# RWKV block times routed experts: rounded count sums, an earlier table load, a split wait, a reordered step

## The reference, cut to what matters

```
xn  = layernorm(x)                                # 8192 tokens of 256 channels, 16 sequences of 512
s   = rwkv_block(xn)                              # time mixing with a decaying state, then channel mixing
g   = silu(moe(xn))                               # 8 experts, top-1024 tokens chosen by each expert
out = x + s * g

# inside rwkv_block, channel mixing
kf  = square(relu(xk2 @ Wfk.T))                   # hidden width 1024
out = x + sigmoid(xr2 @ Wfr.T) * (kf @ Wfv.T)

# inside moe: each expert takes its cap = 1024 most probable tokens
_, top_idx = top_k(softmax(xt @ Wg).T, cap)
h   = gelu(xt @ W1[e]) @ W2[e]
```

## Time and profile before

| | us |
|---|---|
| median of 3 runs | 1070.64 |
| the profiled execution | 1072.04 |
| its span | 1070.3 |
| TensorE busy (matmuls) | 1016.8 (95%) |
| VectorE busy | 875.6 (82%) |
| ScalarE busy | 688.2 (64%) |
| GpSimd busy | 392.4 (37%) |

### The profile page before, as it was taken

The page is one execution under the profiler, slowest core; times in us unless marked ns, Lnnn a source line. Parts: engine busy times, 40 slices in busy tenths (PEclk is TensorE's granted clock), DMA queues, the critical chain, the costliest instruction groups (busy, mean ns, idle before and its releaser), DMA issues.

```text
span 1070.3 us, 18410 instructions
## 1 busy us (share of the span) xinstructions
PE 1016.8 (95%) x5410; PEld 835.7 (78%) x5410; DVE 875.6 (82%) x1750; ACT 688.2 (64%) x1232; POOL 392.4 (37%) x421
## 2 busy tenths in 40 slices
PE   4899999999999999999999899999997999999996
PEld 4668787676877777787786768677786999999985
DVE  5899899998989899898999979787554777777765
ACT  2558566586856768576684847667364666666653
POOL 3204057100001011000200368766515666666653
PEclk9889999999999999999999999999998999999999
DMA  7543320101201011010101102018613333333310
GB/s 257 175 139 119 97 81 21 40 20 41 59 0 59 0 59 58 1 59 0 59 30 30 39 22 60 1 52 250 211 29 93 102 113 113 113 114 110 108 47 22
DMA packets 59474, 80.29 MB, mean 75 GB/s; under 512 B 7678, under 2 KB 46719, under 8 KB 59394
## 3 DMA queue, kind: packets, MB, share of 16 engines
q1 hardware_dynamic: 48130, 54.16, 16.0%
q0 software_dynamic: 11280, 25.32, 8.0%
HBM read 64.38 MB, written 26.36 MB: 85 GB/s over the span
## 4 chain that ended last, share of the span: by engine, by line
PE 67%; ACT 12%; DVE 11%; issue 4%; POOL 3%; another core or an unknown queue 1%; DMA 1%; SPq 0%; ACTq 0%; DVEq 0%; POOLq 0%
PE psKV L1002 18%; PE psM L939 13%; PE psM L1076 11%; PE psM L953 5%; ACT arena L663 3%; ACT arena L560 3%; PE psM L978 2%; PE psM L971 2%; PE psM L973 2%; ACT arena L659 2%; PE psKV L1096 1%; PE psKV L1098 1%; PE psKV L1097 1%; PE psT L904 1%
## 5 line engine op out<-in xcount | busy, mean ns | idle before, releaser
L1002 PE MATMUL psKV<-arena 128*128 128x256 f32 x1024 | 233.3, 383 | 8.9 <-ACT arena L663 8.9
L1002 PEld LDWEIGHTS psKV<-arena 128*128 128x128 f32 x1024 | 193.8, 191 | 50.0 <-issue 22.7
L439 POOL TENSOR_SCALAR lnw<-mv 128x4 f32<-128x4 f32 x32 | 19.4, 608 | 468.7 <-DVE mv L1396 468.7
L1076 PE MATMUL psM<-arena 128*128 128x128 f32 x1136 | 142.4, 279 | 4.7 <-DVE arena L1647 3.4
L1076 PEld LDWEIGHTS psM<-arena 128*128 128x128 f32 x1136 | 134.9, 194 | 6.9 <-DVE arena L1647 4.4
L607 ACT ACTIVATE arena<-psM 128x512 f32<-128x512 f32 x64 | 36.5, 588 | 133.5 <-PE psM L939 133.5
L522 POOL DMA_INDIRECT out_dram<-arena,list_sb x71 | 87.6, 1234 | 74.3 <-issue 41.8
L1413 DVE SCALAR_TENSOR_TENSOR arena<-arena,vecs 128x512 f32<-128x512 f32 x160 | 110.0, 746 | 0.1
L971 PE MATMUL psM<-mix_hi,wfk_hi 128*128 128x512 f32 x256 | 105.5, 412 | 0.2
L973 PE MATMUL psM<-mix_hi,wfk_lo 128*128 128x512 f32 x256 | 100.6, 393 | 0.0
L560 ACT ACTIVATE arena<-s_ring,cf 128x256 f32 (+1 forms) x128 | 66.4, 595 | 47.8 <-POOL cf L444 47.8
(11 more groups left out here) (210 smaller groups left out, 2372.5 us busy)
## 6 DMA issues: line engine op xcount, KB each, us to landing
arena<-in_x SPq DMA_DIRECT2D x16, 512.0 KB
desk<-in_xT SPq DMA_DIRECT2D x16, 512.0 KB, 4.0
xs_rows<-s_ring SPq DMA_DIRECT2D x16, 512.0 KB
xs_rows<-in_x SPq DMA_DIRECT2D x16, 512.0 KB
desk<-in_x SPq DMA_DIRECT2D x15, 512.0 KB, 5.3
desk<-in_W SPq DMA_DIRECT2D x8, 512.0 KB
arena<-in_W SPq DMA_DIRECT2D x8, 512.0 KB, 7.4
out_dram<-arena,list_sb POOLq DMA_INDIRECT x71
```

Of the source, the lines that this page charges most:

```text
L1002: ins = pe.matmul(psKV[:, j // 2, (j % 2) * C:(j % 2 + 1) * C], kf2[:, h, j * P:(j + 1) * P], wfv[:, h, :], start=(h == 0), stop=(h == HC ...
L1076: ins = pe.matmul(psM[:, t % 2, f * P:(f + 1) * P], w1_t[t % 2][:, k, f * P:(f + 1) * P], xnT[t % 2][:, k, :], start=(k == 0), stop=(k == ...
```

## The change

Four edits. The bits' sum is a float32r matmul of a copy of `esum` against two columns: the counts, now written into a float32r tile, and a column of ones that nobody reads. ScalarE does a Tanh of one column into an unread tile straight after the logs. `channel_out(…, 0)` waits for the first four squares before its first matmul and for all eight before its fifth. In the experts' step t = 68 `split_h(70)` comes ahead of `combine(68)` instead of behind it.

```diff
+        unread = sb("unread", [P, 1])
+        esum_r = sb("esum_r", [P, P], F32R)
+        counted = sb("counted", [P, 2], F32R)
...
             def round_(b, ffn=True, ahead=True, softmax=False, further=True, placing=False):
                 logs(b)
+                act.activation(unread[:], ones[:, 0:1], ACT.Tanh)
                 if placing:
                     keep_counts()
...
-                pe.matmul(psR[:, 0:1], esum, tiny[:, 4:5], start=True, stop=True).then_inc(S["bit_summed"], 1)
+                pe.matmul(psR[:, 0:2], esum_r[:], counted[:], start=True, stop=True).then_inc(S["bit_summed"], 1)
...
             def channel_out(b, j):
                 if j == 0:
-                    pe.wait_ge(S["sq_done"], b * HC + HC)
+                    pe.wait_ge(S["sq_done"], b * HC + HC // 2)
...
                 for h in range(HC):
+                    if j == 0 and h == HC // 2:
+                        pe.wait_ge(S["sq_done"], b * HC + HC)
                     ins = pe.matmul(psKV[:, j // 2, (j % 2) * C:(j % 2 + 1) * C], kf2[:, h, j * P:(j + 1) * P],
...
                 if isinstance(b, int) and b == ROUTER_ROUNDS and point == 2:
+                    v.tensor_copy(esum_r[:], esum)
+                    v.tensor_copy(counted[:], ones[:, 0:2])
...
-                v.tensor_scalar(work, selT, cand, None, ALU.is_ge, ALU.add, accum_out=cnt).then_inc(S["bit_counted"], 1)
+                v.tensor_scalar(work, selT, cand, None, ALU.is_ge, ALU.add, accum_out=counted[:, 0:1]).then_inc(S["bit_counted"], 1)
...
+                if t == TILES - 3:
+                    split_h(t + 2, (i + 2) % RING)
                 combine(t, i, g)
-                if t < TILES - 2:
+                if t < TILES - 3:
                     split_h(t + 2, (i + 2) % RING)
```

More of the change, by code:

```diff
@@ L1228, in turned_probabilities @@
                 R.wait()
-            t_f, bit, cand, kept, cnt = (tiny[:, k:k + 1] for k in range(5))
+            t_f, bit, cand, kept = (tiny[:, k:k + 1] for k in range(4))
             def try_bit(b, point):
```

## The result

| | median us | ratio to before, of the means |
|---|---|---|
| before, beside it | 1071.09 (4 runs) | |
| changed | 1059.43 (1055.91 to 1060.07, 4 runs) | 0.9885 [0.9862, 0.9909] |
| changed, second comparison | 1060.0 (6 runs) | 0.9881 [0.9857, 0.9905] |
| changed, third comparison | 1058.53 (6 runs) | 0.9876 [0.9842, 0.9909] |

The change makes the kernel 11.7 us faster by the medians; 13.0 was forecast, and 1057.6 us for what came out at 1059.43. The second and third comparison have 12.0 and 13.0 us (before 1071.97 and 1071.57 there).

The account below looks back on a forecast made before the run. TensorE, 67% of the chain, was taken as the bound; 8.6 + 0.4 - 0.7 + 1.0 - 0.3 + 2.5 + 1.5 = 13.0 us off, 1057.6 us against the median. Own range 1055 to 1060.5; 8 in 10, 1052.5 to 1063.

Parts of the forecast that it names:

- The split wait: At `channel_out`, TensorE's 0.81 us gap before the matmuls goes, with little kept in rounds 3, 11 and 12: 8.6 us gained.
- VectorE's give-back: In seven loop rounds VectorE's residual add holds up `project`'s second block, about 0.1 us each: 0.7 us lost.
- The rival in which only 0.3 us of a round is kept: VectorE's residual add takes over in loop rounds; 5.6 us come back, total 1063; chance 0.18, including a longer table switch.
- waits of L939 (now L943) for L1550 (L1558) over 0.5 us a round: Sign that the forecast is wrong: TensorE's `project` waits for VectorE's residual add over 0.5 us a round.
- The table load: Tanh's load moves behind the logs: 0.4 us gained in rounds 13 and 14, 1.0 in round 15, 0.3 lost in round 0.
- The sums: Each bit's sum on TensorE takes one instruction instead of a pair: 28 x 0.09 = 2.5 us gained.
- The end: In the last tile of the experts, TensorE's last twelve matmuls follow the previous twelve without waiting: 1.5 us gained.
- a round was to take near 44.5 us in the loop and 44.0 in round 13: Sign that the forecast is right: distance between two `receptance` starts near 44.5 us in loop rounds (45.6 before), 44.0 in round 13.

Follow-up runs that it names:

- e2: The kernel before with the early one-column Tanh alone: ratio 0.9987 [0.9977, 0.9998], 1.4 us off 1057.3.
- e6: The changed kernel with a Ln and another Tanh behind the early Tanh, two more table loads a round: 1.0102 [1.0087, 1.0117] against the kernel before.
- e3: The kernel before with the rounded (float32r) bits' sums alone: ratio 0.9975 [0.9965, 0.9986], 2.6 us off 1057.3.
- e4: The kernel before with the reordered experts' step alone: ratio 0.9985 [0.9976, 0.9994], 1.6 us off 1057.3.
- e5: The changed kernel with the split wait undone: ratio 0.9961 [0.9947, 0.9974] to the kernel before.
- e7: The changed kernel with VectorE's residual add ahead of the v half of the time mix in rounds 3 to 12: 0.9859 [0.9844, 0.9874] to before.
- e9: The changed kernel with the residual add first, and the early Tanh behind the copies in rounds 0 and 12: 0.9855 [0.9842, 0.9869] to before.
- e1: The kernel before with the split wait alone: ratio 0.9909 [0.9895, 0.9922], 9.6 us off 1057.3.
- e10: The changed kernel once more, unaltered, in the second comparison: 0.9881 [0.9857, 0.9905] to the kernel before.
- e11: The changed kernel with the residual add ahead of the v-mix in rounds 3 to 12, beside the changed kernel: 0.9867 [0.9845, 0.9889] to before.

## Why the prediction was right

**The split wait, 8.6 us.** Right, and the largest. The gap of 0.81 us goes in full (round 13: 0.87 from transposes to `channel_out`), the second wait finds the squares done, and no extra time shows for the two waits: 16 matmuls take 3.46 us from 652.50 to 655.96, and the same 16 took 3.53 in before. These 0.07 us a round were not counted. Alone it brought 9.6 us, with 8.6 inside its interval (8.2 to 11.1); `project` of k then still takes 3.52 us in the loop rounds, so VectorE takes nothing back. The places where little was to be kept are right too: round 3 gains nothing (47.0 in both; the gap of 1.1 goes and `project` of k takes 4.28 instead of 3.47), round 12 gains 0.1.

**VectorE's give-back, 0.7 us.** The term that was mis-sized most. The mechanism stood in the prediction: TensorE gains more than VectorE's 0.69 us of idle time, and the residual add then follows the v-mix with no gap. It was counted as 0.1 us a round. Measured are 0.33 us at the add and 0.16 at the start of `project`, which the prediction had not looked at: 0.49 us in each of rounds 5 to 10. In round 4 `project` of k takes 3.58 to 3.60, 0.06 to 0.08 more, and the parts lose nothing to each other. So it is about 3.0 us in seven rounds where 0.7 was counted, with 0.8 a round as the bound. The rival in which only 0.3 us of a round is kept did not come: 0.96 is kept. Its sign, waits of L939 (now L943) for L1550 (L1558) over 0.5 us a round, was a poor one: the list shows two such waits, 0.5 and 0.6 us and none of them in the loop, and has the loop's 0.33 us nowhere.

**The table load.** Forecast +0.4 in rounds 13 and 14, 1.0 in round 15, -0.3 in round 0, 0.45 lost in round 12 and nothing in the loop. Measured by e2: 0.5 us in each of rounds 13 and 14 (44.5 and 44.4 against 45.0 and 45.0), 1.4 in round 15, 0.4 lost in round 12 (52.3 against 51.9), and 0.20 in each loop round, 1.4 us in seven. So alone it is worth more than was counted, though half of the loop's part is the gap that the split wait takes anyway; end to end e2 brings 1.4 us [0.2, 2.4]. In round 0 TensorE's router waits 4.0 us for the logits instead of 2.5, as forecast; whether any of it reaches the end is inside the scatter of the start (71.7 to 73.4 us over all kernels with one load). The Tanh follows the new load by 0.01 us (637.83 + 1.28 = 639.11, start 639.12), where the earlier trace rows had 0.02. The Trainium skill (ScalarE: Activation LUTs, What ACT_TABLE_LOAD costs) adds a drain of about 1380 ns to the 1283 ns; the length agrees with the rows, the drain appears in none of them, and the 1.5 us of an extra load with its Tanh in e6 leaves no room for it.

**The sums, 2.5 us.** Right: 0.32 us a round with four bits, 0.08 a bit where 0.09 was taken; e3 brings 2.6 us [1.5, 3.7].

**The end, 1.5 us.** Right: 1.6 us [0.6, 2.5] in e4. From round 15 to the end, on chips where before takes 1057 us, the kernels take 290.6 to 291.0 us with the edit (e4, e5, e6, e7, e9) and 292.4 to 293.2 without it (e1, e2, e3), 1.4 us at the least.

**The sum.** Forecast 13.0; measured 11.7, and 12.0 and 13.0 in the two later comparisons. The mechanisms were right, and that the number came so near is in part luck: two terms were mis-sized and partly cancel. VectorE takes some 2.3 us more than counted. On the other side each loop round gains 0.07 us at `channel_out` and 0.24 inside `hidden`, for which the terms had 0.09, and rounds 13 to 15 gain some 0.9 us more than counted. Over the rounds alone 11.8 us were forecast (13.0 less the 1.5 of the end and the -0.3 of round 0) and 11.8 measured. The four parts' ratios multiply to 0.9857, 15.1 us off 1057.3, against 0.9881 for the mean of the three comparisons; the intervals of these are too wide to show the difference of 2.5 us, the loop rounds' 0.43 us show it. Of the other signs, a round was to take near 44.5 us in the loop and 44.0 in round 13: it takes 44.7 and 43.8.

## What to carry to other kernels

A wait for the last of several producers is worth splitting when the consumer's own first half takes longer than what is missing; then look for the engine that was almost late already, since it takes back part of the gain, and its wait may hide inside a run of instructions that shows none: start to start of the same run in both kernels finds it. Parts measured alone add up to more than the whole where they work on one path; a period between two fixed instructions of a loop resolves 0.02 us where single executions of one kernel spread over 2 to 9. Cutting that period into stretches says which part is counted twice and which is taken back. An order change that frees 0.25 us a round can be lost again in the rounds that differ from the loop, where the work moved off one path stands on another.

## What the runs showed of the hardware that was not expected

**Two kinds of chips.** The same kernel before takes 1070.64 to 1071.97 us in some sessions and 1056.54 or 1057.33 in others. The slower times are from the first comparison and from chips 6 and 11, the faster ones from chips 2 and 4; each chip was used in one session, so that chip and session can't be told apart. The rounds don't differ (round 0 to 15 takes 690.5 us in before there, 690.7 in e4 here); the experts' stage does, 306.9 us against 292.4 to 293.2. In windows of 10 us, first the changed kernel's second execution (1057.8 us of span), then e1 (columns: PE, PEld, DVE, ACT, POOL busy, granted clock, DMA share, GB/s):
```profile
800.00:810.00 10.00, 4.68 (x33) 3.98 (x32) 2.03 (x5) 2.40 (x5) 7.30 (x7) 0.93 0.33 92
810.00:820.00 10.00, 9.09 (x60) 8.69 (x60) 6.62 (x13) 5.62 (x13) 4.97 (x5) 0.73 0.34 102
820.00:830.00 10.00, 10.00 (x91) 10.00 (x90) 7.35 (x15) 6.45 (x16) 6.60 (x7) 1.00 0.36 99
```
```profile
800.00:810.00 10.00, 10.00 (x89) 9.94 (x89) 7.47 (x15) 6.96 (x15) 8.14 (x7) 1.00 0.30 89
810.00:820.00 10.00, 10.00 (x89) 9.94 (x88) 7.72 (x15) 6.79 (x15) 7.71 (x7) 1.00 0.43 132
```
On the slower chips TensorE (here e10) stands still several times a microsecond at a time in one place of the experts' stage, put down to "issue":
```profile
804.83 0.28 PE L1103 MATMUL psKV<-w_lo,hT_h 128*128 x1 [1.05 <-issue]
806.25 0.28 PE L1102 MATMUL psKV<-w_hi,hT_h 128*128 x1 [1.02 <-issue]
807.69 0.37 PE L1103 MATMUL psKV<-w_lo,hT_h 128*128 x1 [0.81 <-issue]
```
and a stretch at the lower of its two levels, 1.2 GHz, follows, from 808.5 to 815.4 us (0.73 on the mean of that window). Both come some 50 us after round 15 in before and changed kernels alike, so they are no part of the change; they differ from execution to execution, though (6.6 to 11.1 us of pauses, as said above), and so scatter the comparison. e1, e2, e4 and e7 have none of these "issue" pauses. What stops the issue there was not tried.

**A late add without a cause.** In some executions VectorE starts the residual add about 1 us after `project_out` has ended while it is idle: in round 14 of the first changed execution (704.32; `project_out` ends at 703.37, the next matmul starts at 703.21; the round took 44.6 us), not in the other two (43.7), and in rounds 13 and 14 of e11, not of e7 with the same code. The trace names no other releaser; it stays open.
